# Quantised feed-forward kernel: weight copies moved behind the splits on ScalarE, one residual moved to VectorE, one accumulator opened a product later

## The reference, cut to what matters

```python
def fp4_quant_dequant(x):                      # along the last dim, blocks of 16
    xb = x.reshape(shape[:-1] + (shape[-1] // BLOCK, BLOCK))
    scale = jnp.max(jnp.abs(xb), axis=-1, keepdims=True) / 6.0
    scale = jnp.maximum(scale, jnp.float32(1e-12))
    idx = jnp.searchsorted(_MID, jnp.abs(xb / scale))
    q = _GRID[idx] * jnp.sign(xb / scale) * scale
def fp4_linear(x, w):
    return jnp.einsum('bsk,nk->bsn', fp4_quant_dequant(x), fp4_quant_dequant(w))
...
x = x + attention(_layernorm(x), ctx, ctx, Wq, bq, Wout, bout)   # autocorrelation, top 12 shifts
n = _layernorm(x)
h = silu(fp4_linear(n, w_gate)) * fp4_linear(n, w_up)
x = x + fp4_linear(h, w_down)
```

## Time and profile before

| | us |
|---|---|
| median of 3 runs | 466.32 (466.32 to 467.92) |
| the profiled execution | 466.81 |
| its span on the core | 465.0 |
| granted TensorE clock, mean | 1.00 |

### The profile page before, as it was taken

How to read it: one execution, slowest core, us unless ns; L and a number is a source line. 1 busy time by engine, 2 the same in 40 slices (tenths; PEclk the granted TensorE clock), 3 DMA queues, 4 the chain that set the end, 5 groups by cost and what they waited for, 6 DMA issues and landing times.

```text
span 465.0 us, 10105 instructions
## 1 busy us (share of the span) xinstructions
PE 443.0 (95%) x3436; PEld 298.7 (64%) x3436; DVE 431.3 (93%) x766; ACT 408.7 (88%) x710; POOL 252.7 (54%) x346
## 2 busy tenths in 40 slices
PE   4889998998989999999999999999999999999997
PEld 4778887755555666666666666666666666666676
DVE  3699979789899999999999999999999999999894
ACT  3369979889999999999999999999999999987684
POOL 4167772573555555666655566666666666433330
PEclk9999999999999999999999999999999999999999
DMA  7999911252446666665666766656656675656653
GB/s 241 339 348 350 357 43 35 69 137 46 90 93 141 140 141 130 149 132 131 131 132 130 137 138 143 141 130 143 142 132 134 139 143 111 128 111 132 122 122 94
DMA packets 162003, 67.95 MB, mean 146 GB/s; under 512 B 126368, under 2 KB 161696, under 8 KB 161952
## 3 DMA queue, kind: packets, MB, share of 16 engines
q1 hardware_dynamic: 161952, 67.31, 61.7%
HBM read 27.38 MB, written 9.18 MB: 79 GB/s over the span
## 4 chain that ended last, share of the span: by engine, by line
PE 68%; ACT 4%; DVE 3%; issue 2%; DVEq 0%; ACTq 0%
PE ps L1083 15%; PE ps L1061 14%; PE ps L1063 14%; PE ps L1062 14%; PE ps L1086 8%; PE ps L1128 2%; ACT h_c L653 1%; ACT h_c L650 1%; DVE y_h L1486 1%; PE ps L947 1%; DVE bm L1511 0%; ACT ps L782 0%; PE ps L1096 0%; ACT a_xT L716 0%; DVE ctx_sb L1380 0%
## 5 line engine op out<-in xcount | busy, mean ns | idle before, releaser
L1061 PE MATMUL ps<-guT_hi,a_xT 128*128 128x512 f16 (+1 forms) x384 | 138.7, 361 | 4.1 <-DVE hb L1375 3.0
L1063 PE MATMUL ps<-guT_hi,a_xT 128*128 128x512 f16 (+1 forms) x384 | 138.7, 361 | 0.0
L1062 PE MATMUL ps<-guT_lo,a_xT 128*128 128x512 f16 (+1 forms) x384 | 138.7, 361 | 0.0
L1083 PE MATMUL ps<-dT_hi,hqT 128*128 128x256 f16 x704 | 124.4, 273 | 0.4 <-ACT ps L782 0.3
L545 POOL TENSOR_TENSOR ctx_sb<-w_q_lo,sl 128x704 f16<-128x704 f16 x60 | 90.2, 1523 | 4.1 <-DVE ctx_sb L1443 4.1
L1086 PE MATMUL ps<-dT_lo,hqT 128*128 128x256 f16 x384 | 87.3, 273 | 0.0
L1083 PEld LDWEIGHTS ps<-dT_hi,hqT 128*128 128x128 f16 x704 | 68.9, 98 | 10.4 <-ACT ps L782 0.7
L599 POOL TENSOR_TENSOR xs<-xs,w_raw 128x512 f32<-128x512 f32 x30 | 38.4, 1279 | 64.2 <-DVE ctx_sb L1380 57.8
L561 POOL TENSOR_TENSOR sl<-bm,sh 128x240 f16<-128x240 f32 (+2 forms) x33 | 31.1, 941 | 74.9 <-DVE y_h L1486 72.0
L711 ACT ACTIVATE w_raw<-ps,inv_gu 128x704 f32<-128x704 f32 x64 | 53.8, 840 | 15.8 <-PE ps L1063 15.6
L1061 PEld LDWEIGHTS ps<-guT_hi,a_xT 128*128 128x128 f16 x384 | 37.6, 98 | 38.6 <-issue 2.7
(11 more groups left out here) (189 smaller groups left out, 813.2 us busy)
## 6 DMA issues: line engine op xcount, KB each, us to landing
xs<-in_x_dram SPq DMA_DIRECT2D x16, 512.0 KB, 8.7
ctx_sb<-in_ctx_dram SPq DMA_DIRECT2D x16, 512.0 KB, 8.3
out_dram<-a_xT SPq DMA_DIRECT2D x64, 128.0 KB, 2.1
w_raw<-a_scratch SPq DMA_DIRECT2D x60, 128.5 KB, 2.7
hqT<-ctx_sb SPq DMA_TRANSPOSE x62, 3.7
w_raw<-in_L_ffn_w_down_dram SPq DMA_DIRECT2D x1, 704.0 KB, 8.1
w_raw<-in_L_ffn_w_gate_dram SPq DMA_DIRECT2D x1, 640.0 KB, 5.1
w_raw<-in_L_ffn_w_up_dram SPq DMA_DIRECT2D x1, 640.0 KB, 6.4
```

Source lines behind the costliest of these rows:

```text
L1061: pe.matmul(dst, xt[:, c, :], guT[0][:, c, n0:n1], start=(c == 0), stop=False)
L1062: pe.matmul(dst, xt[:, c, :], guT[1][:, c, n0:n1], start=False, stop=False)
L1063: last = pe.matmul(dst, xt[:, KC + c, :], guT[0][:, c, n0:n1], start=False, stop=(c == KC - 1))
L1083: last = pe.matmul(dst, hqT[:, j % 4, c, :], dT_hi[:, c, :], start=(c == 0 and not preset(j)), stop=(c == DCH - 1))
```

## The change: what it does

1. On ACT the five copies of the down weights move. Entry 9 stood between `silu(2)` and `silu(3)`, 10 at the end of stage 1, 11 between `silu(4)` and `silu(5)`, 12 before `split_h(1)`. Now 9 stands at the end of stage 1 behind `split_x(3)`, 10 and 11 at the end of stage 2 behind `split_x(4)`, and 12 at the start of stage 3, ahead of `silu(6)`. Entry 8 stays.
2. On PE the transposes of entries 10 and 11 move behind gate 5, that of entry 12 between gates 6 and 7, and the fillers ahead of them go from 12 to 10. The wait for all copies moves from inside gate 6 to the start of `down(0)`.
3. `added(0)` becomes true: tile 0 has no opening and no preset, and its residual runs on DVE in stage 4, directly ahead of that of tile 1. Opening 2 in gate 8 therefore waits for the DVE instruction, where it waited for ACT's.
4. Near the end, opening 61 moves on PE from behind down 58 to behind down 59.

```diff
         def added(i):
-            return i % 4 == 1 and i // 2 < NP - 4
+            return i == 0 or i % 4 == 1 and i // 2 < NP - 4
...
         def n_added(i):
-            return (min(i, 2 * (NP - 4) - 1) + 3) // 4
+            return 1 + (min(i, 2 * (NP - 4) - 1) + 3) // 4
...
                 if st < NP:
+                    if st == 3:
+                        evacuate_weights(act, range(GU_FILLS + 4, len(FILLS)))
                     residuals(2 * st - 8)
                     square_x(st + 4)
                     scale_high(st)
                     residuals(2 * st - 7)
                     silu(2 * st)
                     preset_x(2 * st - 6)
-                    if st <= 2:
-                        evacuate_weights(act, range(GU_FILLS + 2 * st - 1, GU_FILLS + 2 * st))
                     normalise_x(st + 3)
...
                     silu(2 * st + 1)
-                    if st == 2:
-                        evacuate_weights(act, range(GU_FILLS + 4, len(FILLS)))
                     if st < NP - 1:
                         preset_x(2 * st - 5)
                         split_h(j)
                     split_x(n)
                     if st == 1:
-                        evacuate_weights(act, range(GU_FILLS + 2, GU_FILLS + 3))
+                        evacuate_weights(act, range(GU_FILLS + 1, GU_FILLS + 2))
+                    if st == 2:
+                        evacuate_weights(act, range(GU_FILLS + 2, GU_FILLS + 4))
...
-                if i == 6:
-                    pe.wait_ge(s["w_ev"], len(FILLS))
-                if i >= 6:
+                if i >= 8:
                     open_down(i - 6)
...
                     if n == 2:
-                        pe.wait_ge(s["w_ev"], GU_FILLS + 2)
-                        filler(5, 7)
+                        filler(5, 6)
                     gate_and_up(2 * n)
-                    if n == 2:
-                        transpose_weights(GU_FILLS + 3)
+                    if n == 3:
+                        transpose_weights(GU_FILLS + 4)
                     gate_and_up(2 * n + 1)
                 if n == 0:
                     pe.wait_ge(s["w_ev"], GU_FILLS + 1)
                     filler(7, 6)
+                if n == 2:
+                    filler(10, 6)
                     transpose_weights(GU_FILLS + 2)
-                if n == 2:
-                    pe.wait_ge(s["w_ev"], GU_FILLS + 3)
-                    filler(12, 6)
-                    transpose_weights(GU_FILLS + 4)
+                    transpose_weights(GU_FILLS + 3)
+                if n == 3:
+                    pe.wait_ge(s["w_ev"], len(FILLS))
+                if n == NP + 1:
+                    open_down(2 * NP - 3)
                 if tile_ok(2 * n - 6):
                     down(2 * n - 6)
-                if n == NP:
-                    open_down(2 * NP - 3)
...
-                    if tile_ok(2 * st - 7) and added(2 * st - 7):
-                        residual(2 * st - 7)
+                    for i in (2 * st - 8, 2 * st - 7):
+                        if tile_ok(i) and added(i):
+                            residual(i)
```

## The result

| | before | changed |
|---|---|---|
| median us (lowest to highest) | 466.62 (466.29 to 469.32), 22 runs | 468.81 (466.32 to 471.12), 22 runs |
| the profiled execution | 466.81 | 469.57 |
| its span, mean granted clock of TensorE | 465.0, 1.00 | 467.7, 0.993 |

The ratio is 1.0035, 95% interval 1.0022 to 1.0049. The forecast was 466.3 with a range to 467.5; the time is outside it.

The account below looks back on a forecast made before the run. PE and DVE were both taken as full, DVE setting the pace by a hair. The moved residual's -0.29 and the end's +0.27 summed to 0.0 us, so the forecast was the median before, 466.3, range 465.0 to 467.5.

Parts of the forecast that it names:

- the sum: Whole kernel: -0.29 from the moved residual and +0.27 at the end make 0.0 us, so 466.3.
- steady state against before: Stages after stage 4: PE and DVE both stay 0.29 us ahead of before, bounds -0.5 and -0.1.
- Stages 1 to 3: First stages: DVE gains 2.05 us from two vanished waits; ACT's moved copies just fit stage 3, 0.03 us reserve.
- 2.5 or more as a sign: First opening in gate 8: PE waits 2.5 us or more, released by DVE's residual near 140.4.
- The moved residual: Gate 8: opening 2 waits for DVE's residual until 140.4, 0.2 us later than before, delaying later work; worth -0.29.
- the lead of 1.65: DVE after stage 4: 1.65 us ahead, shrinking to 0.29 because it must wait for ACT's split.
- my three conditions for being wrong: PE leaves the first opening before 139.5, DVE has no wait near 149, or down 60 starts before 452.8.
- A rule weighed: Opening 2: whether PE's 2.8 us idle also halves its clock afterwards; the sum took no extra cost.
- the row: Earlier trace's clock windows: granted clock 1.00 even where PE had no instruction, read as idle time costing only itself.
- Slower by the clock: Rival, chance 0.02: half clock from opening 2 through gates 8 and 9 costs 4.6 us more, giving 470.9.
- The end: Last stages: opening 61 comes 1.36 us later, delaying ACT's preset and last split; costs 0.27, bounds 0 and 0.4.
- Down 59's earlier end brings nothing: Last stages: no gain, as down 60 waits for a transpose released by DVE's work; otherwise down to -0.5.

Follow-up runs that it names:

- e9: Changed kernel plus seven filler products in the attention part near 81 us, wait at opening 2 left; 468.36 us, ratio 1.0023.
- e2: Changed kernel with 11 filler products ahead of opening 2, so PE works during the wait; 467.18 us, ratio 1.0013.
- e5: Kernel before with only tile 0's residual moved to DVE, ahead of tile 1's; 470.24 us, ratio 1.0074.
- e1: Changed kernel with DVE's residual of tile 0 moved ahead of the scales of pair 4; 466.28 us, ratio 0.9982.
- e4: Kernel before with opening 61 alone moved behind down 59; 467.09 us, ratio 1.0000.
- e3: e1 with opening 61 back in its old place behind down 58; 465.60 us, ratio 0.9969.
- e7: e6 plus seven filler products in the attention part near 81 us; 465.24 us, ratio 0.9967.
- e8: e3 plus the seven filler products in the attention part near 81 us; 465.68 us, ratio 0.9961.
- e6: Changed kernel with tile 0's residual back on ACT, its opening in gate 7, opening 61 in its old place; 465.45 us, ratio 0.9978.

## Why the prediction was wrong

The profile of e9 is the changed kernel around opening 2 without a fall, so the sum can be held against it. Its `y_h(0)` starts at 108.64, 0.28 after before's, which is taken off.

| step | forecast | e9, less 0.28 |
|---|---|---|
| transpose of entry 12 on PE | 127.44 | 127.44 |
| opening 2 on PE | 140.4 | 140.34 |
| `silu(9)` on ACT | 144.3 | 144.22 |
| `split_h(3)` on ACT | 145.44 | 145.36 |
| `offset_h(3)` on DVE | 149.47 | 149.39 |
| steady state against before | -0.29 | -0.39 (273.39 - 0.28 - 273.50) |
| last transposes on PE | no earlier than 457.6 | 457.66 |

- **Stages 1 to 3: right.** Neither of the first two splits is waited for, and DVE comes to `offset_h(2)` without a wait: stage 3 fits. In e9 PE waits 0.51 us for ACT at the transpose of entry 12 (127.72), as forecast. In the changed profile it waits at gate 6 instead, 1.65 us for a DMA transpose of x (125.05), and comes to entry 12 late enough for the copy to be done. I had no such wait. It makes PE some 0.4 later at gate 8 and so shortens the idle time at opening 2: 2.17 us printed, where I had asked for 2.5 or more as a sign. Why this transpose lands later in some executions is open; it costs nothing, since opening 2 waits for DVE either way.
- **The moved residual: right as far as it went.** Opening 2 at 140.4, the lead of 1.65 shrunk to 0.37, and none of my three conditions for being wrong came true.
- **A rule weighed: this step failed.** I wrote that by the row "the idle time costs only itself", so that the matmuls behind it stood in the sum at nothing extra, and gave the rival "Slower by the clock" 0.02. It is what happened. The changed profile shows half the clock for some 3.4 us from 0.7 us behind the wait, which costs DVE 1.7 us; e2 shows the same wait filled and no fall, e5 shows wait and fall without the copies. The rule of the Trainium skill ("TensorE: Matmul & The Clock Gate", Why this matters for your kernels) names what the trace shows here, 0.50 behind the idle 2.17 us, though it is worded for longer gaps than this one. Nothing fell in the profile of e9, with 2.40 us.
- **The row was misread.** The earlier trace rows give a granted clock of 1.00 for 0 to 5 us, where PE has no instruction. The first matmuls of the same trace tell what the figure is worth:

```profile
6.46 1.09 PE L890 MATMUL ps<-ident,ctx_sb 128*128 128x128 f32 x4 [6.46 <-DMA ctx_sb<-in_ctx_dram]
7.34 1.06 PE L900 MATMUL ps<-ident,xs 128*128 128x128 f32 x4
...
11.10 0.60 PE L900 MATMUL ps<-ident,xs 128*128 128x128 f32 x4
11.54 0.60 PE L890 MATMUL ps<-ident,ctx_sb 128*128 128x128 f32 x4
```

  Four products take 0.86 to 0.88 us from start to start at 6.5 us, and 0.43 to 0.44 at 11 us. They ran at half the clock after the idle start while the view says 1.00. The distance of like matmuls was the evidence for the rule, and it lay in the kernel before. That every later wait had left the clock alone said little: all were shorter, the longest 1.63 us (26.28), and 1.16 near the place in question.
- **The rival's size was off too.** I priced it at 4.6 us, for a fall to the end of gate 9. The stretch ended at about 145.4, 3.4 us long, and half of that is what it took from PE. It costs 1.7 us on DVE: `offset_h(3)` is at 151.10 in the changed profile and at 149.39 in e9.
- **From one fall to the median.** The three executions at full clock had a median of 466.40; 1.7 more would be 468.1, and 9 of 22 have a second stretch or more (0.993 or less) for another 1.3 or so. (That fall cost 1.3: PE's L1017 products at 73.81 were 0.41 earlier than before's, `y_h(0)` 0.91 later.) The median of 468.81 lies between.
- **The end: mechanism right, size in the runs at or above the forecast.** ACT's part came out as worked out (1.36 of delay, +0.22 on DVE's wait against my +0.27). The profile of e9 shows no more than that: its last residual, 462.47 - 0.28, is 0.16 before that of before, after entering 0.39 before it, so +0.23; that of e2 gives +0.24 (0.71 ahead on entering, 0.47 at the last residual). The profiles of e1 and e4 show +0.4, the changed kernel's +0.5, and the times say +0.4 or more (e3, e4). What is above the forecast may be no matter of the opening, since e7 and e8 lose 0.5 with the old end. "Down 59's earlier end brings nothing" held: down 60 waits for its transpose, which also lands later there. In the changed profile SP issues it at 451.69 and PE goes on 4.5 us later; before it was issued at 449.49 and PE started on it at 453.12, 3.6 us. Why the transfer takes longer is open (last section).

**What would be better than both.** The copies' part is worth keeping: e3, e6, e7 and e8 are all faster than the kernel before, by 0.2 to 0.4%. Whether tile 0's residual is on DVE (e3) or on ACT (e6) can't be told in their times, taken on two chips (465.60 and 465.45); where the change put it, it costs (e5). The new opening at the end costs 0.2 to 0.5, and gives nothing back.

## What to carry to other kernels

When an edit lets an engine run ahead and then stand at one wait, price TensorE's clock as well as the wait: behind two idle microseconds the clock fell in more than half of the executions (7 of 12 in e9, by their mean clock), and neither the busy time nor any list of waits on that engine shows it. Look at the distance between like matmuls, not only at the granted clock, before concluding that idle time is free. Either bring the releasing instruction forward, as e1 did, or fill the wait, as e2 did, and look at the spread of the runs: three of 22 executions at the old time were the sign that the sum was right and something happened only sometimes.

## What the runs showed of the hardware

- A fall of the clock isn't a property of a program alone. The same idle place (2.17 and 2.40 us in two profiles) had one and had none. With the fillers near 81 us, 7 of 12 executions had one (e9). The kernel before has one in about a third (25 of 74); where, no profile of it shows, but in e3, which has no long wait and falls once, it is near 81 us, after waits of 0.82, 0.18, 0.18 and 0.67 us. What decides in a given execution is open.
- Seven constant products near 81 us took the executions at full clock from 20 of 36 to 16 of 16.
- In the last stages an instruction transfer of some 16 KB (27 of them make 0.44 MB) can come close to a DMA transpose. DMA packets by queue, changed kernel, 452 to 454 us:

```profile
q1 hardware_dynamic: 505, 0.13, 113.5%
q8 instruction: 1, 0.02, 4.2%
```

  It comes at 452.4 to 452.6, between the issue of the transpose for down 60 (451.69) and its first packets (452.8). The packets almost stop between 453.6 and 454.8, and down 60 starts 4.5 us after the issue, against 3.6 before. In e1, e4 and e9, all with the new end, the order is the same and the time 4.4, 4.0 and 4.0 us; in e7 and e8, with the old end, it happens to the transpose for down 61, which waits 0.59 and 0.56. Before and in e3 and e6 the transfer comes when the packets of both transposes are through or nearly so, and nothing is late. e2 is the exception: the transfer comes at 448.9 to 449.1, between issue (448.77) and first packets (449.9), and down 60 starts 3.6 us after the issue, there bounded by ACT. So the two go together in six of seven profiles. No run moved the transfer alone; whether it is the cause, and why it comes earlier in some kernels, stays open.
